# Cross attention on one core: each step's maximum moved between its scores and its product with the values

## What is computed

```python
hidden = jnp.concatenate([context, latents], axis=1)          # 1601 + 256 keys
q = (latents @ Wq.T)   # 16 heads of 96
k = (hidden @ Wk.T)    # 4 heads of 96, each shared by 4 query heads
v = (hidden @ Wv.T)
attn = jax.nn.softmax(scores, axis=-1)
out = jnp.einsum('bkgqs,bksd->bkgqd', attn, v) @ Wo.T
```

## Time and profile before

| | |
|---|---|
| median of three runs | 1899.72 us (1896.34 to 1900.12) |
| the profiled execution's own time | 1896.53 us |
| its span | 1894.6 us |
| granted TensorE clock over the span | 0.997 |
| PE busy | 1863.6 us, 98% |
| DVE, ACT, POOL busy | 1223.6, 1170.8, 705.7 us |
| attention proper, batch 0 | from 811 to 1012 us; the other batches from 1073, 1335 and 1598 us, some 200 us each |

### The profile page before, as it was taken

One profiled execution on the slowest core, in us unless ns is written; L12 is line 12 of the kernel. 1 busy time (PEld: TensorE's weight loads), 2 busy tenths in 40 slices (PEclk: granted clock), 3 DMA queues, 4 the chain that ended last, 5 costly groups with the idle time before them and its releaser, 6 DMA issues.

```text
span 1894.6 us, 28063 instructions
## 1 busy us (share of the span) xinstructions
PE 1863.6 (98%) x9512; PEld 1536.7 (81%) x9512; DVE 1223.6 (65%) x2111; ACT 1170.8 (62%) x2056; POOL 705.7 (37%) x720
## 2 busy tenths in 40 slices
PE   6999999999999999999999999999999999999998
PEld 5888888888888788977779877779777798777786
DVE  5655656566565731578874688855788746788555
ACT  6666656666566642467776577765677764777621
POOL 5666757667575540301213012103012130123431
PEclk9999999999999999999999999999999999999999
DMA  4001101001010235300111100103001114000220
GB/s 174 29 29 29 45 11 55 28 28 29 26 55 13 79 141 192 87 1 9 29 29 51 45 5 17 28 21 91 1 9 28 29 51 146 26 17 15 86 88 29
DMA packets 59585, 89.86 MB, mean 47 GB/s; under 512 B 7254, under 2 KB 42454, under 8 KB 58720
## 3 DMA queue, kind: packets, MB, share of 16 engines
q1 hardware_dynamic: 59488, 88.57, 14.9%
HBM read 67.52 MB, written 21.03 MB: 47 GB/s over the span
## 4 chain that ended last, share of the span: by engine, by line
PE 55%; DVE 3%; ACT 1%; issue 1%; DMA 0%; SPq 0%; ACTq 0%; POOLq 0%
PE b_o_ps L1269 16%; PE b_s L1256 16%; PE b_s L1211 7%; PE b_s L1207 6%; PE b_m L1227 5%; PE b_m L1292 4%; DVE b_pr L1092 2%; PE b_s L1313 1%; DVE b_mx L1481 1%; ACT b_pf L1392 0%; ACT b_pr L1086 0%; PE b_x L1238 0%; DMA a_hid<-x_t 0%; PE b_x L1301 0%; PE b_s L1326 0%
## 5 line engine op out<-in xcount | busy, mean ns | idle before, releaser
L1269 PE MATMUL b_o_ps<-b_pr,b_v 128*97 128x512 f32 (+1 forms) x1440 | 376.1, 394 | 3.8 <-DVE b_pr L1092 3.0
L1256 PE MATMUL b_s<-b_q,b_kt 97*128 97x512 f32 (+1 forms) x1440 | 375.0, 394 | 0.0
L1092 DVE TENSOR_TENSOR b_pr<-b_pf,b_pr 128x1024 fp32r<-128x1024 f32 (+1 forms) x256 | 318.2, 1243 | 68.1 <-ACT b_pr L1086 68.0
L1481 DVE TENSOR_REDUCE b_mx<-b_m 128x1 f32<-128x1024 f32 (+1 forms) x256 | 286.7, 1120 | 110.6 <-PE b_m L1227 110.3
L1392 ACT ACTIVATE b_pf<-b_s 128x1024 f32<-128x1024 f32 (+1 forms) x256 | 247.9, 969 | 121.7 <-PE b_s L1256 121.6
L1269 PEld LDWEIGHTS b_o_ps<-b_pr,b_v 128*97 128x97 f32 (+1 forms) x1440 | 230.9, 162 | 104.6 <-issue 14.4
L1256 PEld LDWEIGHTS b_s<-b_q,b_kt 97*128 97x128 f32 (+1 forms) x1440 | 262.1, 185 | 62.3 <-issue 0.8
L1086 ACT ACTIVATE b_pr<-b_pf 128x1024 fp32r<-128x1024 f32 (+1 forms) x256 | 257.6, 1006 | 46.9 <-PE b_o_ps L1269 43.2
L1606 POOL TENSOR_TENSOR b_y<-b_recs,b_o 96x512 f32<-96x512 f32 x32 | 41.5, 1296 | 638.8 <-ACT b_recs L1419 638.8
L445 PE MATMUL a_ring<-a_xt,w_a 128*128 128x512 f32 x1128 | 276.9, 396 | 0.0
L445 PEld LDWEIGHTS a_ring<-a_xt,w_a 128*128 128x128 f32 x1128 | 207.0, 189 | 40.6
(11 more groups left out here) (123 smaller groups left out, 2640.6 us busy)
## 6 DMA issues: line engine op xcount, KB each, us to landing
hraw<-in_ctx_t SPq DMA_DIRECT2D x92, 128.0 KB, 2.5
raw_a<-in_w_qkv SPq DMA_DIRECT2D x30, 384.0 KB, 3.3
raw_a<-in_w_o SPq DMA_DIRECT2D x32, 256.0 KB, 3.0
queries<-a_q SPq DMA_DIRECT2D x24, 256.0 KB, 2.0
b_qraw<-queries SPq DMA_DIRECT2D x16, 384.0 KB, 3.8
attended<-b_y SPq DMA_DIRECT2D x32, 192.0 KB, 2.1
y_first<-attended SPq DMA_DIRECT2D x4, 1536.0 KB, 7.0
x_t<-a_xt SPq DMA_DIRECT2D x2, 2048.0 KB, 8.4
```

The costliest lines, as they stand in the source:

```text
L1092: dve.tensor_tensor(pr[0:rows, k % 2, LO, 0:n], pf[0:rows, k % 2, 0:n], f(pr[0:rows, k % 2, HI, 0:n]), ALU.subtract).then_inc(p_lo.sem, 1)
L1256: mm = pe.matmul(ps_s[k % 2][0:rows, i * BANK:(i + 1) * BANK], kt[:, kv, a, t0:t0 + rows], q[:, kv % 2, m, hp * BANK:(hp + 1) * BANK], sta ...
L1269: mm = pe.matmul(ps_o[0:HD2 + 1, :], v[0:rows, slot(g // 2), a, t, :], pr[0:rows, k % 2, m, i * BANK:(i + 1) * BANK], start=t == 0 and s = ...
L1481: dve.reduce_max(mx[:, g % 2, t, half:half + 1], ps_m[:, 0:MAXW[half][1]], X).then_inc(mx_made.sem, 1)
```

## The change

In steps j = 1 to 6 of groups 0 to 6, the maximum product goes in front of the values product instead of behind it.

```diff
         step = [("scores", k)] + [("pv", k - 2)] * (k >= 2)
-        s += step if j else step[::-1]
+        between = [("max", g + 1, j + 1)] * (more and j < PAIRS - 1)
+        s += step[:1] + between + step[1:] if j else step[::-1] + between
         if more and j == PAIRS - 1:
             s += [("row", g + 1)]
-        if more and j < PAIRS - 1:
-            s += [("max", g + 1, j + 1)]
```

## The result

The changed kernel takes 1917.46 us (median of 4 runs, 1914.77 to 1918.68), the kernel before 1899.72 (4 runs). The ratio is 1.0101, with an interval of 1.0087 to 1.0116: slower by 1%, well clear of the 0.2% that can be told. The prediction was 1917. Its profiled execution took 1918.12 us, with a span of 1916.3, 21.7 above the span before.

A forecast was written before the change was run, and what follows sets the result against it. PE, busy for 98% of the span, was taken as the bound. The terms, 4.8 + 4.5 + 7.8 + 3.3 - 1.2 - 0.3 = 18.9 us, gave 1915.4 or 1918.6 by baseline; forecast 1917, range 1907 to 1926.

The forecast's parts named there:

- 1, product 2 in groups 1 to 6: In step 1 the maximum product directly follows the scores: 0.09 late plus 0.11, 24 places by 0.20, 4.8 us.
- 2, product 3 in groups 1, 3, 5, 6: Reduction 2 still stands behind the first low part on DVE: 0.17 late plus 0.11, 16 places, 4.5 us.
- 3, product 3 in groups 2, 4: Low part takes 1.93 while POOL splits queries: 0.87 late plus 0.11, 8 places, 7.8 us, the largest single price.
- 4, product 3 in group 0: The first values product is moved behind it: 0.71 late plus 0.11, 4 places, 3.3 us.
- Term 5: Values products less late: 1.2 us gained in groups 2 and 4, 0.3 in the last batch; bounds 3.0 us and nothing.
- The 0.05 and the 0.11: At a batch's start: product starts 0.05 us after its reduction, then takes 0.57 instead of 0.46, a further 0.11.
- The rival that named no change: "Nothing": stalls early in a group are given back later in it, 1896 to 1903 us; chance 3%.
- All other steps free: Remaining steps cost nothing: 0.8 us left over, thinnest behind step 3's sums, reduction 5 through at 851.6, product 6 wanted 852.0.
- The rule against the row: Slow start of 0.11 us in 52 stalls, 5.7 us, kept against the skill's reorder window, which would give 1911.
- The signs that I named: PE's busy time within a few us of 1863.6; b_m waits from 8 to 60 or so; products 2 and 3 late.
- Shorter stalls: PE restarts without the 0.11, or groups 2 and 4 meet POOL at another moment and pay 0.28; 1904 to 1911, 8%.
- Faster: All 13 values-product waits for the low part go, some 4 us with slow starts; 1891 to 1895, 3%.

The follow-up runs named there:

- Half reductions: Each maximum reduction reads only the first half of its columns: 1891.52 us in the old order (ratio 0.998), 1901.93 us in the new order (1.0028).
- the swapped queue: Changed kernel, but in step 1 of each group DVE does reduction 2 ahead of the low part instead of behind it: 1927.78 us, one run.
- the old step 1: Changed kernel, but step 1 as before (values product, then maximum product), the new order only from step 2 on: 1918.5 us (ratio 1.0117).
- the run with steps 4 to 6 alone: New order only in steps 4 to 6, steps 1 to 3 as in the kernel before: 1911.93 us (ratio 1.0078).
- the run with the queries moved: Changed kernel, with POOL's split of the queries in groups 2 and 4 moved from step 2 to step 5: 1917.39 us (ratio 1.0111).

## Why the prediction was right

The mechanism was right, and so was the total. How exactly the numbers meet is luck: errors of up to 1.9 us in the last terms cancel, the runs themselves spread from 1914.8 to 1918.7, and the two medians differ by 17.7 where the groups' sum has 19.3. Term by term, the lateness of starts plus the slow second matmul, from the timeline of the changed kernel:

| term | places | predicted | measured |
|---|---|---|---|
| 1, product 2 in groups 1 to 6 | 24 | 4.8 | 4.6 (0.09 + 0.10) |
| 2, product 3 in groups 1, 3, 5, 6 | 16 | 4.5 | 4.3 (0.16 + 0.11) |
| 3, product 3 in groups 2, 4 | 8 | 7.8 | 7.8 (0.87 + 0.11) |
| 4, product 3 in group 0 | 4 | 3.3 | 3.1 (0.66 + 0.11) |
| product 4 in groups 2, 4 | 8 | 0 | 0.6 |
| 5, values products in groups 2, 4 | 8 | -1.2 | -1.2 |
| 5, boundary behind groups 3, 5 | 6 | 0 | -1.9 |
| 5, last batch: product 7 less the values product | 3 | -0.3 | +1.6 |
| sum | | 18.9 | 18.9; groups' sum 19.3 |

**Terms 1 to 4** stand. The 0.05 and the 0.11, read from two places at a batch's start, held in the new ones: none of the 71 starts less than 0.05 after its reduction's end, 64 of them within 0.06. That DVE's reduction 2 would not come forward is seen in the start 1.15 after the low part, in both kernels. Half reductions, the swapped queue and the old step 1 confirm it from three sides.

**Term 5** was wrong in two parts that cancel. For the last batch I laid out the low part but took ACT's delay (the two copies, the weights' high part, then the high part of step 4) too short; product 7 is 0.9 late and not 0.25. At the boundary I said the wait would stay, since the low part moves with its values product. It does, but POOL's work does not move with it, and holds the low part less: counted from the group's first scores, the low part of step 6 starts 0.46 later than before and POOL's last piece ends only 0.13 later.

Both errors are of one kind: the other engines do not move by the same amount as PE. In group 2 of the last batch, ACT's two copies come 0.69 later than before, since the exponent ahead of them waits for scores that the new order and its early stalls have moved by 1.09; the sums on DVE, which release the copies, come only 0.1 later. The high part and the low part then come 0.69 late too.

The upper end for this term was wrong as well. I took it from the 3.0 us of the earlier trace rows, but the values products became less late by some 4.5 us (1.2, 1.9 and 1.4 of the last batch). The 13 waits of the earlier trace rows are six at the boundaries, four behind group 6 and three in the last batch; the eight late products in groups 2 and 4 are not among them, since their 0.11 is hidden in the listed length of the matmul ahead. The rival that named no change leaned on the same 3.0 us.

**All other steps free.** Right but for product 4 in groups 2 and 4, whose reduction ends just as it is wanted (0.08 each); there is no wait at products 5 and 6, so the 0.35 us that I left behind the sums was there. The run with steps 4 to 6 alone shows how thin: with product 5 at its old, later start the same place stalls 0.52 us, the lateness that the same arithmetic gave (852.0 against 851.5).

**The rule against the row.** The Trainium skill, page "TensorE: Matmul & The Clock Gate", in the table at its head, says that the queue pulls weight loads ahead of matmuls that are under way. Taken as the prediction takes it, that would have left out the 0.11. Here the load waited too: all 71 waits stand on the weight load, which starts together with the first matmul (854.60 and 854.61 in the run with steps 4 to 6 alone), and the blocks of products 2 and 3 then take 0.57 where an unstalled one takes 0.46. In the kernel the wait for the reduction stands ahead of the load, a case that the table's row does not speak of. For such a stall the measurement decides for the row of the trace; why the second matmul comes 0.11 late was not tested.

**The signs that I named.** The places held, and nearly the count: 71 for "60 or so", the other eleven being product 4 in groups 2 and 4 and product 7 in the last batch. That PE's busy time would stay within a few us was wrong: it rose by 14.3. Of that, 3.1 us lie ahead of the attention, where the lower clock was granted for longer, and 11.3 inside it: so more than half of the 19.3 us is hidden in the listed length of PE's matmuls. A reader who had trusted the 98% would have seen no stall.

**The rivals.** "Shorter stalls" (1904 to 1911) is where another kernel lands, the one with POOL's instructions in pieces, at 1909.3, by the second of the ways named there. "Faster" had its deciding number right: 1.94 against 1.85. With half reductions (0.69) the loop is 1.40, product 2 doesn't wait, and even then the new order loses 10 us.

## What to carry to other kernels

Two engines that hand one buffer back and forth have a loop time (here 0.66 + 1.23 + 0.05 us); the work between two uses on the other engine must be longer, and moving an operation from behind a block to in front of it takes that block out of the loop once, at the seam where the new order starts. Look at the seam and at every step where the partner engine carries something extra, not at the steady step: here the steady step had 0.8 us to spare and nearly all of the 19 us came from two products per group. When one engine's stalls are moved by an experiment, give the price of the place they land in with the same care as the gain.

## What had not been expected of the hardware

- A low part on DVE that begins while POOL runs an elementwise instruction is held for the rest of it: 3.15 us instead of 1.23 in the run with the queries moved. It ends 1.08 us after the POOL instruction, in 676 of 726 places. Four pieces instead of one instruction brought the first low part of groups 2 and 4 from 1.93 to 1.29 us.
- Of TensorE's clock: behind 1.6 us of idle time in the run with the swapped queue, the granted clock of the next 2.7 us was 0.51, the 1.2 GHz level, and a values product took 2.63 instead of 1.39. The level fell behind such an idle time in three of eight places, and what set the three apart was not found. The waits of up to 1.2 us on the weight load in the changed kernel had no such effect: the window of the whole attention of batch 0 has a granted clock of 1.00.
- Profiles of kernels with the same code ahead of the cross attention differ by up to 5.5 us in when it begins. In the two compared here the first 50 us had a granted clock of 0.97 and 0.86, and it began 2.4 us later in the second. The twelve begin in the order of their time at the lower level, but not every run was profiled, so that this makes the whole spread between runs was not tested.
